# A mixture-of-experts block with two layer norms: the normalising of the second norm is split into a row of subs and a row of muls, with the expert's output matmuls between them

## The chip, the cores and the metric

The kernel runs on the 8 NeuronCores of one Trainium2 chip (trn2). Each core computes 4096 of the 32768 tokens; the cores don't exchange data. The metric is the device time of the slowest core in microseconds (us).

## The reference

Inputs: x of 4 x 8192 x 1024, attention weights of 1024 x 1024, a router of 8 x 1024, w1 (1024 x 8192) and w2 (8192 x 1024) of 8 experts.

```python
xp = x @ Wp.T + bp
q, k, v = (xp @ W.T + b for each, 16 heads of 64; q scaled)
# each token attends to itself and its two neighbours (i-1, i, i+1 modulo s)
x = layernorm(x + (softmax(q . k_neighbours) v_neighbours) @ Wo.T + bo)
# experts: sigmoid router, top 2 of 8, weights normalised to sum 1
h = einsum('td,edw->etw', xf, W1e)
a = square(relu(h))
y = einsum('etw,ewd->etd', a, W2e)
out = einsum('etd,te->td', y, cw)
x = layernorm(x + out)
```

## The kernel before, in words

Everything is feature-major: a tile has 128 partitions of features and 512 columns of tokens, and 8 such chunks (NCH) make up the 1024 features. The kernel has three parts: the weights Wp and Wq, Wk, Wv are multiplied together; eight slabs of 512 tokens go through attention and the first norm, whose result (r1n) is stored to HBM; then come the experts with the second norm, the part that the change touches.

The experts run in NPASS = 4 passes of PW = 1024 tokens, each of NTT = 2 tiles of 512 tokens (`tt` 0 and 1). In a pass the loop goes over 8 experts `e` and the 2 tiles. For each (e, tt) the code writes, in this order:

- on TensorE, the gate matmul (L1038), which spreads this expert's gate over all partitions, and 64 matmuls of h (L1051): 8 chunks, each a sum over 8 matmuls, into two PSUM banks in turn (`ps_hh`);
- on ScalarE, the relu of each chunk (L1058) into one of two buffers of `t1u`; on VectorE the product with the gate (L1063) and with the relu itself (L1067) into `a_sb`;
- then `emit_y` of the *previous* (e, tt): 64 matmuls (L880) with w2, 8 chunks into two PSUM banks in turn (`ps_yy`). For each chunk VectorE copies it to `y_acc` (L889, for e = 0) or adds it (L892), which frees the bank.

The weights of one expert are in `w1e` and `w2e`, 2 MB each in SBUF, one buffer each. `stream_w2(e)` follows the emit_y of the last tile of expert e-1, `stream_w1(e + 1)` follows the h of the last tile of expert e. Both are issued by GpSimd (POOL), which first waits until all earlier loads of its own have landed (`ldb`).

The second norm of a pass is not done at its end. It is cut into pieces that are put in a list, `ln2_pending` (L1103 to L1107), and each (e, tt) of the next pass takes one group off it:

- at (e 0, tt 0), behind emit_y of the last tile of the old pass: `seg_ln2_a` of tile 0 (VectorE adds the residual to y_acc, L912; ScalarE casts it, L918; TensorE sums it with a vector of ones, L923; VectorE squares the cast, L927; TensorE sums the squares, L932; eight times) and `seg_ln2_b_chain` (mean, variance and reciprocal root on one partition: L943 to L949 on VectorE, L954 to L961 on ScalarE);
- at (e 0, tt 1): `seg_ln2_b_bcast` of tile 0 (two matmuls, L968 and L972, spread mean and root over the partitions; ScalarE copies them to `ln2mb`, L978 and L980), `seg_ln2_c` of tile 0 (for each of 8 chunks on VectorE a sub, L995, y_acc less mean into `ln2t`, and a mul, L1000, into `otok`; then SyncE issues the 2 MB store, L1009), `seg_ln2_a` and the chain of tile 1; only then emit_y of (e 0, tt 0);
- at (e 1, tt 0): broadcast and `seg_ln2_c` of tile 1, and then emit_y of (e 0, tt 1).

The norm of the last pass follows behind the last emit_y, with nothing beside it.

Each engine executes its instructions in the order in which the code writes them. emit_y for e = 0 overwrites y_acc of a tile, so it waits until the sub of that tile and chunk has read it (L883 to L886). At the end of expert 1, `load_slice` puts the load of the next pass's r1n (2 MB, L160 on SyncE) behind the stores in SyncE's queue; it waits until they have landed. Pass 3 has no next slice. Before every VectorE instruction that touches a tensor which an earlier one wrote, the helper `_maybe_drain` puts a drain.

I call the three places where a new pass begins turns. At the first one tile 0 is at 1748 us of the trace.

Of the kernel before, what the change touches and what calls it, by code (L numbers as in the profile page):

```python
# [8 lines left out]
BF16 = mybir.dt.bfloat16  # L9
# [5 lines left out]
NCH = 8  # L15
# [3 lines left out]
TT = 512  # L19
# [79 lines left out]
def build_program(T):  # L99
# [3 lines left out]
    PW = T // NPASS  # L103
    NTT = PW // TT
# [40 lines left out]
    p = _Prog(block)  # L145
# [47 lines left out]
    psb = lambda name, shape, dt: ph.enter_context(nc.sbuf_tensor(name, shape, dt)).ap()  # L193
# [16 lines left out]
    for xi, (wxt_h, c_sb, cb_sb, scale) in enumerate(  # L210
# [4 lines left out]
        for dc in range(NCH):  # L215
            for jg in range(2):
# [3 lines left out]
                for kc in range(NCH):  # L220
# [3 lines left out]
                             lambda En, o=role.t, l=lhs, r=rhs, a=(kc == 0), b=(kc == NCH - 1):  # L224
# [5 lines left out]
                          lambda En, o=dst, i_=role.t, sc=scale:  # L230
# [3 lines left out]
        for jc in range(NCH):  # L234
            psfb.wait_writer(p)
            p.wait("tensor", s_ld, base_ld)
            for kc in range(NCH):
                lhs = wxt[:, kc * 1024 + jc * 128: kc * 1024 + jc * 128 + 128]
                v = p.do("tensor",
                         lambda En, o=psfb.t, l=lhs, r=bpb[:, kc:kc + 1],  # L240
                         a=(kc == 0), b=(kc == NCH - 1):
# [5 lines left out]
                      lambda En, o=cb_sb[:, jc:jc + 1], i_=psfb.t, bb=bcol, sc=scale:  # L247
# [469 lines left out]
    ln2scr = psb("ln2scr", [128, 2 * 512], BF16)  # L717
    ln2bc = psb("ln2bc", [128, 2 * 512], BF16)
    ln2mb = psb("ln2mb", [128, 2 * 512], BF16)
    ln2t = psb("ln2t", [128, 2 * 512], BF16)  # L720
    tpk = psb("tpk", [128, 32], F32)
    selp = psb("sel_sb", [E, E * 128], BF16)
    ps_gb = _PsumRole(pst("ps_gb", [128, 512], F32))
# [134 lines left out]
    def stream_w2(e):  # L858
        ldb()
        if w_free[1] is not None:  # L860
            p.wait("gpsimd", *w_free[1])
        dma("gpsimd", w2e.rearrange("p (c n) -> p c n", n=1024),
            w2[e * 1024:(e + 1) * 1024, :].rearrange("(c p) n -> p c n", p=128),
            s_ld, writes=[_h(w2e)])
        return s_ld.n
# [117 lines left out]
        ps_b[2].consumed(s_act, va)  # L983
        ln2st["v_mb"] = va

    def seg_ln2_c(Hh_, tt):
        tok0 = Hh_ * PW + tt * TT
        p.wait("vector", s_act, ln2st["v_mb"])
        if otok_free[0] is not None:
            p.wait("vector", *otok_free[0])  # L990
        for dc in range(NCH):
            ysrc = y_acc[:, dc * PW + tt * TT: dc * PW + tt * TT + TT]
            t_ = ln2t[:, (dc % 2) * 512:(dc % 2) * 512 + 512]
            v_sub = p.do("vector",
                         lambda En, o=t_, a=ysrc: En.tensor_sub(o, a, ln2mb[:, 0:512]),  # L995
                         reads=[_h(y_acc), _h(ln2mb)], writes=[_h(ln2t)], inc=s_dve)
            ln2_freed[(tt, dc)] = (v_sub, ln2st["v_casts"])
            p.do("vector",
                 lambda En, o=otok[:, dc * 512:(dc + 1) * 512], a=t_:
                 En.tensor_mul(o, a, ln2mb[:, 512:1024]),  # L1000
                 reads=[_h(ln2t), _h(ln2mb)], writes=[_h(otok)], inc=s_dve)
        v_otok = s_dve.n
        ln2mb_guard[0] = v_otok
        p.wait("sync", s_dve, v_otok)
        p.do("sync",
             lambda En,
             o=out_h.rearrange("p (c t) -> p c t", t=T)[:, :, tok0: tok0 + TT],
             i_=otok[:, 0:NCH * 512].rearrange("p (c t) -> p c t", t=512):
             En.dma_start(out=o, in_=i_),  # L1009
             inc=s_hw, inc_by=16)  # L1010
        state["n_store"] += 1
        otok_free[0] = (s_hw, s_hw.n)
# [7 lines left out]
    for Hh in range(NPASS):  # L1020
        rp = Hh % 2
        v_w1 = stream_w1(0)
        if Hh == 0:
            v_w2 = stream_w2(0)
            pending = None
        v_h_last = 0
        for e in range(E):
            for tt in range(NTT):
                tok0 = Hh * PW + tt * TT
                apar = (e * NTT + tt) % 2  # L1030
                gbank = ps_gb if apar == 0 else ps_b[0]
                gbank.wait_writer(p)
                if e == 0 and tt == 0:
                    p.wait("tensor", s_dve, gates_ready[Hh])
                v_gb = p.do("tensor",
                            lambda En, o=gbank.t, l=selp[:, e * 128:(e + 1) * 128],
                            r=gates[:, tok0: tok0 + TT]:
                            En.matmul(o[:], l, r, start=True, stop=True), inc=s_pe)  # L1038
                p.wait("tensor", s_ld, v_w1)
                if a_free[apar] is not None:  # L1040
                    p.wait("vector", *a_free[apar])
                for hdc in range(NCH):
                    role = ps_hh[hdc % 2]
                    role.wait_writer(p)
                    for kc in range(NCH):
                        lhs = w1e[:, kc * 1024 + hdc * 128: kc * 1024 + hdc * 128 + 128]
                        rhs = r1n_ps[:, rp * NCH * PW + kc * PW + tt * TT: rp * NCH * PW + kc * PW + (tt + 1) * TT]
                        v = p.do("tensor",
                                 lambda En, o=role.t, l=lhs, r=rhs,
                                 a=(kc == 0), b=(kc == NCH - 1):  # L1050
                                 En.matmul(o[:], l, r, start=a, stop=b),  # L1051
                                 inc=(s_pe if kc == NCH - 1 else None))
                    p.wait("scalar", s_pe, v)
                    t1 = t1u[:, (hdc % 2) * 512:(hdc % 2) * 512 + 512]
                    u = t1u[:, 1024 + (hdc % 2) * 512: 1024 + (hdc % 2) * 512 + 512]
                    if t1_free[hdc % 2] is not None:
                        p.wait("scalar", *t1_free[hdc % 2])
                    va = p.do("scalar", lambda En, o=t1, i_=role.t: En.activation(o, i_[:], AF.Relu),  # L1058
                              reads=[_h(role.t)], writes=[_h(t1u)], inc=s_act)
                    role.consumed(s_act, va)  # L1060
                    p.wait("vector", s_act, va)
                    p.wait("vector", s_pe, v_gb)
                    p.do("vector", lambda En, o=u, a=t1, gb_=gbank.t: En.tensor_mul(o, a, gb_[:]),  # L1063
                         reads=[_h(t1u), _h(gbank.t)], writes=[_h(t1u)], inc=s_dve)
                    vb = p.do("vector",
                              lambda En, o=a_sb[:, apar * NCH * 512 + hdc * 512: apar * NCH * 512 + (hdc + 1) * 512],
                              a=u, b=t1: En.tensor_mul(o, a, b),  # L1067
                              reads=[_h(t1u)], writes=[_h(a_sb)], inc=s_dve)
                    t1_free[hdc % 2] = (s_dve, vb)
                gbank.consumed(s_dve, vb)  # L1070
                if tt == NTT - 1:
                    v_h_last = s_pe.n
                prev = pending
                boundary = (prev is not None and prev[5] == E - 1
                            and prev[3] == NTT - 1)
                if boundary:
                    emit_y(prev)
                    w_free[1] = (s_pe, s_pe.n)
                    v_w2 = stream_w2(0)
                if ln2_pending:  # L1080
                    for f in ln2_pending.pop(0):
                        f()
                if prev is not None and not boundary:
                    emit_y(prev)
                    if prev[5] == e - 1 and prev[3] == NTT - 1 and e > 0:
                        w_free[1] = (s_pe, s_pe.n)
                        v_w2 = stream_w2(e)
                pending = (apar, vb, v_w2, tt, Hh, e)
            if e == 1 and Hh + 1 < NPASS:
                if Hh >= 1:  # L1090
                    slice_guard[(Hh + 1) % 2] = [(s_pe, h_done[Hh - 1]),
                                                 (s_dve, r2_done[Hh - 1])]
                load_slice(Hh + 1)
            if e == 3 and Hh + 1 < NPASS:
                seg_router(Hh + 1)
                gates_ready[Hh + 1] = s_dve.n
            if e + 1 < E:
                w_free[0] = (s_pe, v_h_last)
                v_w1 = stream_w1(e + 1)
        h_done[Hh] = v_h_last  # L1100
        w_free[0] = (s_pe, v_h_last)
        mk = lambda fn, tt: (lambda Hh_=Hh, tt_=tt: fn(Hh_, tt_))
        ln2_pending = [[mk(seg_ln2_a, 0), mk(seg_ln2_b_chain, 0)]]  # L1103
        for t_ in range(1, NTT):
            ln2_pending.append([mk(seg_ln2_b_bcast, t_ - 1), mk(seg_ln2_c, t_ - 1),
                                mk(seg_ln2_a, t_), mk(seg_ln2_b_chain, t_)])
        ln2_pending.append([mk(seg_ln2_b_bcast, NTT - 1), mk(seg_ln2_c, NTT - 1)])  # L1107
    emit_y(pending)
    pending = None
    for grp in ln2_pending:  # L1110
        for f in grp:
            f()

    p.wait("sync", s_hw, s_hw.n)
# [74 lines left out]
```

How the kernel before makes its waits and increments, by code:

```python
    def wait(self, eng, sem, val):  # L39
        if val <= 0:
            return
        self.ops[eng].append(lambda E, s=sem, v=val: E.wait_ge(s.h, v))
# [10 lines left out]
    def do(self, eng, fn, reads=(), writes=(), inc=None, inc_by=1):  # L53
        self._maybe_drain(eng, tuple(reads), tuple(writes))
        if inc is None:
            self.ops[eng].append(lambda E, f=fn: f(E))
        else:
            inc.n += inc_by
            self.ops[eng].append(lambda E, f=fn, s=inc, k=inc_by: f(E).then_inc(s.h, k))
        for h in writes:
            self.dirty[eng].add(id(h))
        for h in reads:
            self.read[eng].add(id(h))
        return inc.n if inc is not None else None
```

## Time and profile before

| | us |
|---|---|
| median of 2 runs | 3494.83 |
| the two runs | 3466.35 and 3523.31 |
| profiled execution | 3476.52 |
| its span, slowest core (4) | 3475.0 |
| spans of the eight cores | 3446.3 to 3475.0 |
| TensorE busy | 2780.9 (80%) |
| VectorE busy | 1506.9 (43%) |
| ScalarE busy | 784.8 (23%) |

The span goes from the first to the last instruction of a core; the time holds 1.5 us more around it. PE is TensorE, DVE is VectorE, ACT is ScalarE, POOL is GpSimd, SP is SyncE. A row of a timeline has the start and the length in us, engine, line, operation, the tensor written and those read, how many were merged, and in brackets how long the engine stood idle before it and what released it.

### The profile page before, as it was taken

What the parts mean: (1) busy time and instruction counts of PE and PEld (TensorE: products, weight loads), DVE (VectorE), ACT (ScalarE), POOL (GpSimd) and SP (SyncE); (2) the same over time, 40 slices, a digit from 0 to 9 for tenths busy, and PEclk for the clock granted to TensorE, in tenths of its full rate; (3) what the DMA queues carried; (4) which work ended last, traced back from release to release, by engine and by line L of the source; (5) the groups of instructions that cost most, each with busy time, mean ns of one, the idle gap of its engine ahead of it and who ended that gap; (6) DMA issues with size and microseconds to landing.
All of it is one profiled execution on the core that took longest, in us unless ns stands there. A gap on an engine that the chain in (4) does not pass through costs nothing.

```text
span 3475.0 us, 43311 instructions; the slowest of 8 cores (3446.3 to 3475.0 us)
## 1 busy us (share of the span) xinstructions
PE 2780.9 (80%) x13408; PEld 1288.5 (37%) x13600; DVE 1506.9 (43%) x2794; ACT 784.8 (23%) x1379; POOL 89.4 (3%) x127
## 2 busy tenths in 40 slices
PE   3577778777876499899868989967989986999992
PEld 1255435443542144344323434423434432444440
DVE  0002443344336344444464444455444446444445
ACT  1134334433442111111221111121111112111111
POOL 1000000000000000000000000000000000000000
PEclk9788888887886699999979999978999997999985
DMA  3410100110000533252425524433325242442511
GB/s 51 73 19 13 25 13 13 25 25 13 13 19 13 109 60 63 49 96 51 73 49 108 86 49 70 77 73 87 59 49 95 51 73 49 93 78 50 86 35 49
DMA packets 98764, 189.71 MB, mean 55 GB/s; under 512 B 3256, under 2 KB 11448, under 8 KB 98544
## 3 DMA queue, kind: packets, MB, share of 16 engines
q0 software_dynamic: 77744, 153.38, 26.4%
q1 hardware_dynamic: 20800, 33.56, 3.0%
q8 instruction: 119, 1.95, 0.2%
q14 instruction: 101, 0.83, 0.1%
HBM read 315.05 MB, written 25.17 MB: 98 GB/s over the span
## 4 chain that ended last, share of the span: by engine, by line
PE 55%; DMA 23%; DVE 8%; issue 5%; ACT 4%; DVEq 2%; ACTq 1%; POOLq 0%; POOL 0%; SPq 0%
PE ps_y L880 19%; PE ps_h L1051 16%; DMA w2e<-w 11%; PE ps_mm L401 10%; DMA w1e<-w 8%; PE ps_mm L551 3%; PE ps_f L225 3%; DVEq L49 2%; DMA xbt<-xs 2%; PE ps_s L445 2%; DVE y_acc L912 1%; DVE otok L1000 1%; ACT wbe L503 1%; DVE ln2t L995 1%; ACT ln2scr L918 1%
## 5 line engine op out<-in xcount | busy, mean ns | idle before, releaser
L880 PE MATMUL ps_y<-a_sb,w2e 128*128 128x512 bf16 x4010 | 916.7, 387 | 98.0 <-DMA w2e<-w 41.8
L1051 PE MATMUL ps_h<-r1n_ps,w1e 128*128 128x512 bf16 x4014 | 915.4, 387 | 34.4 <-DMA w1e<-w 25.4
L1058 ACT ACTIVATE t1u<-ps_h 128x512 bf16<-128x512 f32 x512 | 305.6, 597 | 1544.1 <-PE ps_h L1051 1487.4
L880 PEld LDWEIGHTS ps_y<-a_sb,w2e 128*128 128x128 bf16 x4096 | 405.0, 99 | 604.2 <-issue 166.4
L1051 PEld LDWEIGHTS ps_h<-r1n_ps,w1e 128*128 128x128 bf16 x4096 | 402.0, 99 | 534.3 <-issue 95.5
L892 DVE TENSOR_TENSOR y_acc<-y_acc,ps_y 128x512 f32<-128x512 f32 x448 | 307.6, 687 | 471.4 <-PE ps_y L880 462.8
L1063 DVE TENSOR_TENSOR t1u<-t1u,ps_gb 128x512 bf16<-128x512 bf16 x256 | 176.0, 687 | 238.5 <-ACT t1u L1058 236.9
L1063 DVE TENSOR_TENSOR t1u<-t1u,ps_b 128x512 bf16<-128x512 bf16 x256 | 175.9, 687 | 193.8 <-ACT t1u L1058 193.1
L1067 DVE TENSOR_TENSOR a_sb<-t1u 128x512 bf16<-128x512 bf16 x512 | 217.6, 425 | 47.9 <-issue 0.9
L551 PE MATMUL ps_mm<-k_sb,wot_sb 128*128 128x512 bf16 x496 | 137.8, 442 | 34.1 <-DVE pscr L524 27.2
L225 PE MATMUL ps_f<-wxt_sb,wp_sb 128*128 128x512 bf16 x376 | 89.3, 400 | 85.2 <-DMA wxt_sb<-wqt 48.1
L519 DVE TENSOR_TENSOR pscr<-wbe,v_sb 128x512 bf16<-128x512 bf16 x64 | 26.8, 418 | 262.5 <-ACT wbe L503 262.5
L923 PE MATMUL ps_b<-ln2scr,onesv 128*1 128x512 bf16 x64 | 36.7, 574 | 128.7 <-ACT ln2scr L918 128.7
L401 PE MATMUL ps_mm<-x_fm,ckt 128*128 128x257 bf16 x1024 | 119.0, 275 | 14.5 <-ACT k_sb L407 14.0
L401 PE MATMUL ps_mm<-x_fm,cvt 128*128 128x257 bf16 x1024 | 116.9, 273 | 0.5 <-ACT v_sb L407 0.3
L401 PE MATMUL ps_mm<-x_fm,cqt 128*128 128x257 bf16 x1024 | 116.6, 273 | 0.3 <-ACT q_sb L407 0.3
L401 PEld LDWEIGHTS ps_mm<-x_fm,ckt 128*128 128x128 bf16 x1024 | 92.9, 98 | 41.3 <-issue 19.5
L401 PEld LDWEIGHTS ps_mm<-x_fm,cvt 128*128 128x128 bf16 x1024 | 91.6, 97 | 24.5 <-issue 1.3
L401 PEld LDWEIGHTS ps_mm<-x_fm,cqt 128*128 128x128 bf16 x1024 | 91.5, 97 | 24.1 <-issue 0.5
L551 PEld LDWEIGHTS ps_mm<-k_sb,wot_sb 128*128 128x128 bf16 x512 | 55.8, 109 | 116.1 <-issue 71.6
L434 DVE TENSOR_TENSOR pscr<-q_sb,k_sb 128x512 bf16<-128x512 bf16 x128 | 51.4, 422 | 86.4 <-ACT q_sb L407 55.6
L225 PEld LDWEIGHTS ps_f<-wxt_sb,wp_sb 128*128 128x128 bf16 x384 | 38.9, 102 | 134.3 <-issue 93.9
(153 smaller groups left out, 1665.0 us busy)
## 6 DMA issues: line engine op xcount, KB each, us to landing
w1e<-w POOLq DMA_DIRECT2D x32, 2048.0 KB, 14.7
w2e<-w POOLq DMA_DIRECT2D x32, 2048.0 KB, 15.2
out<-otok SPq DMA_DIRECT2D x8, 2048.0 KB, 7.2
xbt<-xs POOLq DMA_DIRECT2D x32, 256.0 KB, 3.8
r1n_hbm<-r1n_stg SPq DMA_DIRECT2D x8, 1024.0 KB, 5.1
r1n_ps<-r1n_hbm SPq DMA_DIRECT2D x4, 2048.0 KB, 15.8
wp_sb<-wp POOLq DMA_DIRECT2D x1, 2048.0 KB, 16.7
wxt_sb<-wqt POOLq DMA_DIRECT2D x1, 2048.0 KB, 17.4
```

Source lines behind the costliest of these rows:

```text
L49: self.ops[eng].append(lambda E: E.drain())
L225: En.matmul(o[:], l, r, start=a, stop=b),
L401: En.matmul(o[:, 0:w_], l, r, start=a, stop=b),
L434: En.tensor_mul(o_, a, b),
L445: En.matmul(ot[0:NH, :], l, r, start=a, stop=b),
L551: En.matmul(o[:], l, r, start=a, stop=b),
L880: En.matmul(o[:], l, r, start=a, stop=b),
L892: va = p.do("vector", lambda En, o=ydst, i_=role.t: En.tensor_add(o, o, i_[:]), reads=[_h(role.t), _h(y_acc)], writes=[_h(y_acc)], inc=s_dve)
L1051: En.matmul(o[:], l, r, start=a, stop=b),
L1058: va = p.do("scalar", lambda En, o=t1, i_=role.t: En.activation(o, i_[:], AF.Relu), reads=[_h(role.t)], writes=[_h(t1u)], inc=s_act)
L1063: p.do("vector", lambda En, o=u, a=t1, gb_=gbank.t: En.tensor_mul(o, a, gb_[:]), reads=[_h(t1u), _h(gbank.t)], writes=[_h(t1u)], inc=s_dve)
L1067: a=u, b=t1: En.tensor_mul(o, a, b),
```

## The change

`seg_ln2_c` becomes two functions: `seg_ln2_c_subs` writes all 8 subs into `ln2t`, which grows from 2 to 8 chunks for it, and `seg_ln2_c_muls` writes the 8 muls and the store. A group of `ln2_pending` becomes a pair: `pre` is written ahead of emit_y (broadcast and subs), `post` behind it (muls and store; for tile 0 also the statistics and the chain of tile 1). At (e 0, tt 0) the group stays whole and stays behind the emit_y of the old pass. The wait for the store that last used `otok` moves from the subs to the muls.

```diff
-    ln2t = psb("ln2t", [128, 2 * 512], BF16)
+    ln2t = psb("ln2t", [128, 8 * 512], BF16)
...
-    def seg_ln2_c(Hh_, tt):
-        tok0 = Hh_ * PW + tt * TT
+    def seg_ln2_c_subs(Hh_, tt):
         p.wait("vector", s_act, ln2st["v_mb"])
-        if otok_free[0] is not None:
-            p.wait("vector", *otok_free[0])
         for dc in range(NCH):
...
-            t_ = ln2t[:, (dc % 2) * 512:(dc % 2) * 512 + 512]
+            t_ = ln2t[:, dc * 512:(dc + 1) * 512]
...
+    def seg_ln2_c_muls(Hh_, tt):
+        tok0 = Hh_ * PW + tt * TT
+        if otok_free[0] is not None:
+            p.wait("vector", *otok_free[0])
+        for dc in range(NCH):
             p.do("vector",
...
-                if ln2_pending:
-                    for f in ln2_pending.pop(0):
-                        f()
+                for f in pre:
+                    f()
                 if prev is not None and not boundary:
                     emit_y(prev)
...
+                for f in post:
+                    f()
...
+        ln2_pending = [([mk(seg_ln2_a, 0), mk(seg_ln2_b_chain, 0)], [])]
         for t_ in range(1, NTT):
+            ln2_pending.append(([mk(seg_ln2_b_bcast, t_ - 1), mk(seg_ln2_c_subs, t_ - 1)],
+                                [mk(seg_ln2_c_muls, t_ - 1),
+                                 mk(seg_ln2_a, t_), mk(seg_ln2_b_chain, t_)]))
+        ln2_pending.append(([mk(seg_ln2_b_bcast, NTT - 1), mk(seg_ln2_c_subs, NTT - 1)],
+                            [mk(seg_ln2_c_muls, NTT - 1)]))
```

TensorE in the kernel before, at a turn, from the broadcast of tile 0 (L968) on; the pair L923, L932 stands there eight times, and L880 is emit_y of (e 0, tt 0):

```order
L968 MATMUL ps_b<-stb,onescol 128x512
L972 MATMUL ps_b<-stb,onescol 128x512
L923 MATMUL ps_b<-ln2scr,onesv 1x512
L932 MATMUL ps_b<-ln2bc,onesv 1x512
...
L880 MATMUL ps_y<-a_sb,w2e 128x512 x64
L1038 MATMUL ps_gb<-gates,sel_sb 128x512
L1051 MATMUL ps_h<-r1n_ps,w1e 128x512 x64
```

The same place after the change (L1042 and L1055 are the old L1038 and L1051):

```order
L968 MATMUL ps_b<-stb,onescol 128x512
L972 MATMUL ps_b<-stb,onescol 128x512
L880 MATMUL ps_y<-a_sb,w2e 128x512 x64
L923 MATMUL ps_b<-ln2scr,onesv 1x512
L932 MATMUL ps_b<-ln2bc,onesv 1x512
...
L1042 MATMUL ps_gb<-gates,sel_sb 128x512
L1055 MATMUL ps_h<-r1n_ps,w1e 128x512 x64
```

emit_y has moved ahead of the statistics matmuls of tile 1, which now stand directly before the h of expert 1. On TensorE nothing else has moved.

VectorE before, at tile 0 of a turn; L995 and L1000 are sub and mul, eight times in turn, L912 and L927 the statistics of tile 1:

```order
L1067 TENSOR_TENSOR a_sb<-t1u 128x512
L995 TENSOR_TENSOR ln2t<-y_acc,ln2mb 128x512
L1000 TENSOR_TENSOR otok<-ln2t,ln2mb 128x512
...
L912 TENSOR_TENSOR y_acc<-y_acc,r1n_ps 128x512
L927 TENSOR_TENSOR ln2bc<-ln2scr 128x512
```

VectorE there after the change (L1071 is the old L1067, L992 the sub, L1004 the mul):

```order
L1071 TENSOR_TENSOR a_sb<-t1u 128x512
L992 TENSOR_TENSOR ln2t<-y_acc,ln2mb 128x512 x8
L889 COPY y_acc<-ps_y 128x512 x8
L1004 TENSOR_TENSOR otok<-ln2t,ln2mb 128x512 x8
L912 TENSOR_TENSOR y_acc<-y_acc,r1n_ps 128x512
L927 TENSOR_TENSOR ln2bc<-ln2scr 128x512
```

The eight copies of emit_y, which stood behind the statistics and the chain of tile 1, are now between subs and muls. At tile 1 it is likewise subs, copies, muls, and then the products of the next h (L1067); before it was subs and muls in turn, copies, products. The orders of ScalarE, GpSimd and SyncE are the same before and after.

## Rows read from the trace of the kernel before

**Rows 1.** The chain that ended last, by engine.

```profile
PE 55%; DMA 23%; DVE 8%; issue 5%; ACT 4%; DVEq 2%; ACTq 1%; POOLq 0%; POOL 0%; SPq 0%
```

**Rows 2.** Timeline of TensorE, first turn, tile 0.

```profile
1748.08 0.39 PE L968 MATMUL ps_b<-stb,onescol 1*128 1x512 bf16 x1
...
1764.22 0.58 PE L923 MATMUL ps_b<-ln2scr,onesv 128*1 128x512 bf16 x1 [15.54 <-ACT ln2scr L918]
...
1780.70 15.82 PE L880 MATMUL ps_y<-a_sb,w2e 128*128 128x512 bf16 x62 [0.33 <-issue]
...
1810.69 0.39 PE L968 MATMUL ps_b<-stb,onescol 1*128 1x512 bf16 x1
```

**Rows 3.** Timeline of VectorE, first turn, tile 0: first sub, first statistics add.

```profile
1750.28 0.68 DVE L995 TENSOR_TENSOR ln2t<-y_acc,ln2mb 128x512 bf16<-128x512 f32 x1
...
1762.63 0.68 DVE L912 TENSOR_TENSOR y_acc<-y_acc,r1n_ps 128x512 f32<-128x512 f32 x1
```

**Rows 4.** Timeline of TensorE, first turn, tile 1 and what follows.

```profile
1811.23 3.63 PE L880 MATMUL ps_y<-a_sb,w2e 128*128 128x512 bf16 x16
1826.07 1.44 PE L880 MATMUL ps_y<-a_sb,w2e 128*128 128x512 bf16 x3 [11.22 <-DVE y_acc L889]
...
1838.07 0.38 PE L1038 MATMUL ps_b<-gates,sel_sb 8*128 8x512 bf16 x1
1838.39 13.99 PE L1051 MATMUL ps_h<-r1n_ps,w1e 128*128 128x512 bf16 x62
1859.36 15.94 PE L880 MATMUL ps_y<-a_sb,w2e 128*128 128x512 bf16 x63 [6.99 <-DMA w2e<-w]
...
1875.55 13.99 PE L1051 MATMUL ps_h<-r1n_ps,w1e 128*128 128x512 bf16 x63
```

**Rows 5.** Timeline of VectorE, first turn, tile 1.

```profile
1812.89 0.68 DVE L995 TENSOR_TENSOR ln2t<-y_acc,ln2mb 128x512 bf16<-128x512 f32 x1
...
1825.24 1.47 DVE L889 COPY y_acc<-ps_y 128x512 f32<-128x512 f32 x2
...
1838.42 0.69 DVE L889 COPY y_acc<-ps_y 128x512 f32<-128x512 f32 x1 [1.04 <-PE ps_y L880]
```

**Rows 6.** Stretches: PE, PEld, DVE, ACT, POOL busy, granted clock, DMA share, GB/s.

```profile
1815.00:1819.00 4.00, 0.00 (x0) 0.00 (x0) 3.54 (x6) 0.00 (x0) 0.00 (x0) 1.00 0.00 0
1819.00:1829.00 10.00, 2.71 (x6) 1.05 (x8) 6.88 (x11) 0.00 (x0) 0.00 (x0) 0.50 0.24 88
```

**Rows 7.** Timeline of TensorE, first turn, behind the statistics of tile 0.

```profile
1731.01 0.60 PE L1038 MATMUL ps_b<-gates,sel_sb 8*128 8x512 bf16 x1
...
1737.63 10.52 PE L1051 MATMUL ps_h<-r1n_ps,w1e 128*128 128x512 bf16 x47 [1.43 <-ACT t1u L1058]
```

**Rows 8.** SyncE's issues and all DMA issues of 1820:1900 with us to landing.

```profile
1825.41 0.58 SPq L1009 DMA_DIRECT2D out<-otok  x1
1833.64 0.57 SPq L160 DMA_DIRECT2D r1n_ps<-r1n_hbm  x1
...
out<-otok SPq DMA_DIRECT2D x1, 2048.0 KB, 8.1
r1n_ps<-r1n_hbm SPq DMA_DIRECT2D x1, 2048.0 KB, 14.3
w2e<-w POOLq DMA_DIRECT2D x1, 2048.0 KB, 20.4
w1e<-w POOLq DMA_DIRECT2D x1, 2048.0 KB, 13.0
```

**Rows 9.** DMA issues of 2968:2990, third turn, with us to landing.

```profile
w2e<-w POOLq DMA_DIRECT2D x1, 2048.0 KB, 15.5
w1e<-w POOLq DMA_DIRECT2D x1, 2048.0 KB, 15.2
```

**Rows 10.** GpSimd's issue of w1e in the first turn, with us to landing.

```profile
1748.93 0.87 POOL L160 DMA_DIRECT2D w1e<-w  x1 [34.77 <-PE ps_b L972]
...
w1e<-w POOLq DMA_DIRECT2D x1, 2048.0 KB, 14.9
```

More of the change, by code:

```diff
@@ L997, in seg_ln2_c @@
             ln2_freed[(tt, dc)] = (v_sub, ln2st["v_casts"])
+    def seg_ln2_c_muls(Hh_, tt):
[3 more added lines that the diff above has]
+        for dc in range(NCH):
             p.do("vector",
-                 lambda En, o=otok[:, dc * 512:(dc + 1) * 512], a=t_:
+                 lambda En, o=otok[:, dc * 512:(dc + 1) * 512],
+                 a=ln2t[:, dc * 512:(dc + 1) * 512]:
                  En.tensor_mul(o, a, ln2mb[:, 512:1024]),
@@ L1075, in build_program @@
                             and prev[3] == NTT - 1)
+                pre, post = ln2_pending.pop(0) if ln2_pending else ((), ())
                 if boundary:
@@ L1102, in build_program @@
         mk = lambda fn, tt: (lambda Hh_=Hh, tt_=tt: fn(Hh_, tt_))
-        ln2_pending = [[mk(seg_ln2_a, 0), mk(seg_ln2_b_chain, 0)]]
+        ln2_pending = [([mk(seg_ln2_a, 0), mk(seg_ln2_b_chain, 0)], [])]
         for t_ in range(1, NTT):
-            ln2_pending.append([mk(seg_ln2_b_bcast, t_ - 1), mk(seg_ln2_c, t_ - 1),
-                                mk(seg_ln2_a, t_), mk(seg_ln2_b_chain, t_)])
-        ln2_pending.append([mk(seg_ln2_b_bcast, NTT - 1), mk(seg_ln2_c, NTT - 1)])
+            ln2_pending.append(([mk(seg_ln2_b_bcast, t_ - 1), mk(seg_ln2_c_subs, t_ - 1)],
[3 more added lines that the diff above has]
+                            [mk(seg_ln2_c_muls, NTT - 1)]))
     emit_y(pending)
     pending = None
-    for grp in ln2_pending:
-        for f in grp:
+    for pre, post in ln2_pending:
+        for f in pre:
+            f()
+        for f in post:
             f()
```

## Prediction

> **What bounds the kernel now.** I read the page's chain of waits first, then the timelines of TensorE, VectorE and SyncE around one turn from a pass of experts to the next, then the DMA issues there. In the chain [rows 1] the reader is to see that TensorE's own work is 55% and DMA 23%: the kernel is an alternation of matmuls and weight loads, and VectorE is on the chain with only 8%. That 8% is the second layer norm. There are four passes. The norm of each of the first three is worked off at the start of the next pass, that of the last at the end. The edit changes the order of instructions only in the three turns. In the last norm it only sorts the same 16 VectorE instructions of a tile otherwise, with nothing beside them.
>
> I call a broadcast (L968) the start of a tile's normalising. For tile 0 [rows 2] TensorE issues it at 1748.08, then stands almost still: 15.54 us before the first statistics matmul of tile 1, and only at 1780.70 does it start emit_y of expert 0. The next broadcast, of tile 1, is at 1810.69, so this stretch takes 62.6 us. VectorE [rows 3] works through 16 subs and muls from 1750.28 to 1762.63: 12.35 us, 0.77 us each. For tile 1 [rows 4] TensorE does two chunks of emit_y (3.63 us), finds both PSUM banks full, and waits 11.22 us for VectorE's y_acc copy, which stands behind another 16 subs and muls [rows 5].
>
> **Tile 0, part by part.** The same 16 instructions exist after the change, each writing a tensor used by the one before it, so I keep 0.77 us for each; splitting them into 8 subs and 8 muls is 6.2 us and 6.2 us. Counted from the broadcast:
> TensorE starts emit_y at 0.6 and fills two banks by 4.2. The subs begin at 2.2 and end at 8.4. The first copy then frees a bank 0.8 us later (1825.24 to 1826.07, rows 4 and 5), so TensorE goes on at 9.2. The other six chunks took 12.0 us after such a wait (1826.07 to 1838.07) [rows 4]; at full speed they are six eighths of 13.99 us, 10.5. I take 12.0, since the wait of 5 us left over is near the point at which the clock falls: in tile 1 the granted clock was 1.00 up to 1819, 4 us into a wait, and then 0.50 (1.2 GHz) for 10 us [rows 6]. TensorE is through at 21.2, the last copy at 22.3 (it starts 0.35 after the matmul, rows 5, and takes a slot of 0.77). The muls end at 28.5.
> Then comes what now follows the muls, the statistics of tile 1: 1762.63 to 1780.70, 18.1 us, to 46.6. Behind it the h matmuls run cold and their relu stands behind ScalarE's four small operations of chain. The trace has exactly that sequence after tile 0's statistics: from the gate matmul at 1731.01, with a wait of 1.43, to the broadcast at 1748.08, 17.1 us [rows 7]. Sum 63.7, against 62.6 before: **1.0 us lost**, in each of three turns 3.0. The 8 subs hidden under emit_y are paid back because emit_y no longer covers chain and the cold clock. If the clock stays up in emit_y, 0.5 is gained instead.
>
> **Tile 1.** The same steps bring TensorE through emit_y at 21.2 after the broadcast, where it was at 27.4 (1838.07 less 1810.69): 6.2 us earlier. The muls are now ahead of the next h phase on VectorE, for 6.2 us. There the relu may run two chunks ahead, so TensorE loses some 1.7 us (two chunks of 1.75 and two of relu against 6.2 and the backlog). That is hidden: the h phase is followed by a wait for w2e anyway, 6.99 us here [rows 4], which h at 14.0 + 1.7 doesn't fill.
>
> So what counts is the chain of transfers: emit_y frees w2e, POOL loads it (and issues the next w1e only when it has landed), and the next h waits for w1e. Here lies the cost that isn't in the code. Before, the store of the outputs was issued at 1825.41, landed after 8.1 us, and the load of the next slice followed at 1833.64, still ahead of w2e at 1838.7 [rows 8]. w2e then took 20.4 us against 15.5 us in the third turn, where no slice is loaded [rows 9]: a transfer beside it cost 4.9. After the change w2e is issued 21.8 us after the broadcast and the store at 28.5, when the muls end: the whole 2 MB store now falls inside w2e's load, and the slice load, which stands behind the store in SyncE's queue, falls on the w1e load.
> - Store beside w2e: between 0 (the store waits) and 8.1 us (w2e waits for all of it); I take 4.5, near the 4.9 of the slice. w2e lands 20.0 after its issue.
> - Slice beside w1e: w1e alone takes 15.2 [rows 9]. The slice began 5 us ahead of w2e and cost it 4.9; begun together the two share for longer. Bounds 0 and 14.3 (the slice's own time, rows 8); I take 7.
> First and second turn, from the end of emit_y to the h matmuls of expert 2: before 1838.07 to 1875.55, 37.5 us. After: 0.6 + 20.0 + 1.0 (issue) + 15.2 + 7 = 43.8, 6.3 more. Less the 6.2 gained, 0.1 lost; and that h runs cold after a wait of some 8 us (12.0 less 10.5 above), 1.5 more: **1.6 lost**, twice 3.2. Third turn: 6.2 less 4.5 for the store: **1.7 gained** (w1e's load is as before).
> Sum: 3.0 + 3.2 - 1.7 = 4.5 us slower, on 3476.5 us of the profiled execution (span 3475.0): **3481 us**. That lies inside the two runs shown (3466 and 3523, median 3494.8), and 0.13% is far below the 2% that a measurement of this kernel can tell from no change.
>
> **The page's rules against this.** The slice row shows that two transfers of different queues share: both moved, both were late. The Trainium skill (DMA: Bandwidth & Descriptors, Queues, rings and completion order) says that each DMA engine takes turns between queue rows, packet by packet. By it the store would cost w2e no more than the store's own share, which is between my bounds; the trace agrees with the 4.9 us.
> A second result: w2e is now issued just ahead of the 8 muls, and POOL writes its descriptors while VectorE reads two SBUF operands. If that held the load up for as long as the muls last, each turn would lose 6.2 us more, 18.6 in all. The only row on it is w1e's load at 1748.9, issued 1.4 us ahead of the same subs and muls: it landed after 14.9 us [rows 10], no later than w1e's 15.2 without them. So I give it little. The Trainium skill (SBUF — State Buffer, Who interferes with whom) states that a VectorE instruction with two SBUF inputs contends with a GpSimd instruction that reads SBUF, though not with one that only writes; the row speaks against a cost here.
>
> **The rivals.**
> 1. Nothing collides, faster. Store and slice find room, the clock stays up: tile 0 gains 3 x 0.5, tile 1 3 x 6.2, together 20.1, so 3456 us; with the 4.9 of w2e's old delay recovered twice (and 37.5 before against 0.6 + 15.5 + 1.0 + 15.2 = 32.3), up to 10 more, 3446. For it: DMA is idle for long stretches, and 11.22 us of wait are plainly visible. Against: the store's issue time follows from the order, 6.7 us into a load of 15.5.
> 2. The pile-up decides, slower. SyncE issues the slice at about the moment POOL issues w1e, after the store and w2e landed together. If w1e gets nothing until the slice is through, it takes 14.3 + 13.0 = 27.3 (rows 8), 5.1 more than I took, twice; with the store at 5.5 instead of 4.5, three more: 4.5 + 10.2 + 3 = 17.7, 3494 us. It decides from the point at which the store lands before w2e does. Against: in rows 8 two loads finished 11 us apart, so both made way.
> 3. Descriptors held up by the muls: 4.5 + 18.6 = 23.1, 3500 us. Against: rows 10.
> 4. The edit does nothing, because VectorE in its order is the only bound: 3476.5. It is within 5 us of my forecast and can't be told from it by time, only by the waits.
>
> **How the numbers follow.** Forecast 0.55 (with rival 4 in it), rival 1 0.2, rival 2 0.2, rival 3 0.05. The cases lie between 3446 and 3500; each carries the scatter of the executions, of which two and the profiled one span 3466 to 3523. Range 3450 to 3512: it holds all the cases but the end of rival 1, and leaves out the top of the scatter. 2% would be 70 us, which no case reaches: within 2% 0.94; slower 0.04, for scatter on rivals 2 and 3; faster 0.02.
>
> **What would show it.** Right: in each turn the wait for y_acc L889 about 5 us instead of 11, and now also in tile 0 (six such waits, three before); 24 to 26 us of TensorE at rest or in statistics after emit_y of tile 0; broadcast to broadcast 62 to 64 us; w2e(1) landing after about 20 us in all three turns; w1e(2) after 20 us or more in the first two, with TensorE waiting 6 to 9 us for it. Wrong: if w2e(1) lands after 15.5 us beside the store, or w1e(2) after 13 to 15 beside the slice (rival 1 then); if w1e(2) takes 27 (rival 2); if w2e(1) starts moving only when the muls have ended (rival 3); if subs in a row take less than 0.77 us each.

## The result and the profile after

The changed kernel takes 3476.5 us (median of 15 runs), the kernel before 3467.0 us (median of 14 runs, the two shown above among them). The ratio is 1.0028, 95% interval 1.0019 to 1.0037: 9.7 us slower, 6.6 to 12.8. That is clear of noise and far below 2%. In some executions of either kernel one die shows a lower granted clock and takes longer; the ratio leaves these out, 3523.3 was one, and the profiled execution before leans that way (cores 4 to 7: clock 0.879, 3464 to 3475 us; cores 0 to 3: 0.884, 3446 to 3457 us). So 3467, close to the lower of the two runs shown above, is the time to start from, and not 3494.8 or 3476.5.

The profiled execution after has a span of 3471.5 us on core 2. Its waits of TensorE, in us in total, times, longest:

```profile
PE ps_b L923 <- ACT ln2scr L918: 108.2, 64, 15.5
...
PE ps_y L880 <- DMA w2e<-w: 40.5, 19, 5.3
PE ps_h L1055 <- DMA w1e<-w: 35.2, 21, 5.9
PE ps_y L880 <- DVE y_acc L889: 31.2, 6, 5.6
```

The wait for the copy is there six times, each of 5 us, instead of three times 11.22 [rows 4]: as forecast, in sum almost the same. TensorE now also waits for w1e, up to 5.9 us on this core and up to 13.1 us on core 7.

Timeline of TensorE on core 2 in the first turn after, from the broadcast of tile 0 on (statistics matmuls left out):

```profile
1751.39 0.39 PE L968 MATMUL ps_b<-stb,onescol 1*128 1x512 bf16 x1
...
1751.93 3.63 PE L880 MATMUL ps_y<-a_sb,w2e 128*128 128x512 bf16 x15
1760.69 12.67 PE L880 MATMUL ps_y<-a_sb,w2e 128*128 128x512 bf16 x47 [5.14 <-DVE y_acc L889]
...
1798.39 0.60 PE L1042 MATMUL ps_gb<-gates,sel_sb 8*128 8x512 bf16 x1
1798.92 5.44 PE L1055 MATMUL ps_h<-r1n_ps,w1e 128*128 128x512 bf16 x16
1805.09 10.52 PE L1055 MATMUL ps_h<-r1n_ps,w1e 128*128 128x512 bf16 x47 [0.72 <-ACT t1u L1062]
1815.54 0.38 PE L968 MATMUL ps_b<-stb,onescol 1*128 1x512 bf16 x1
...
1824.84 13.02 PE L880 MATMUL ps_y<-a_sb,w2e 128*128 128x512 bf16 x47 [5.14 <-DVE y_acc L889]
1837.79 0.38 PE L1042 MATMUL ps_b<-gates,sel_sb 8*128 8x512 bf16 x1
1838.11 7.08 PE L1055 MATMUL ps_h<-r1n_ps,w1e 128*128 128x512 bf16 x32
1846.91 7.07 PE L1055 MATMUL ps_h<-r1n_ps,w1e 128*128 128x512 bf16 x31 [1.72 <-ACT t1u L1062]
1859.30 16.31 PE L880 MATMUL ps_y<-a_sb,w2e 128*128 128x512 bf16 x63 [5.32 <-DMA w2e<-w]
1875.54 0.39 PE L1042 MATMUL ps_gb<-gates,sel_sb 8*128 8x512 bf16 x1
1881.83 15.30 PE L1055 MATMUL ps_h<-r1n_ps,w1e 128*128 128x512 bf16 x63 [5.90 <-DMA w1e<-w]
```

There are three things to see. emit_y of tile 0 stands ahead of the statistics, with its wait of 5.14. The h that follows the statistics (1798.39 to 1815.54, 17.2 us) is the slow one, as in [rows 7]; the granted clock is 0.68 from 1798.4 to 1805 and 1.00 after it. And the two waits for transfers stand behind tile 1.

The DMA issues of that turn after on core 2, with us to landing, which answer to [rows 8]:

```profile
w2e<-w POOLq DMA_DIRECT2D x1, 2048.0 KB, 20.6
out<-otok SPq DMA_DIRECT2D x1, 2048.0 KB, 16.7
w1e<-w POOLq DMA_DIRECT2D x1, 2048.0 KB, 21.7
r1n_ps<-r1n_hbm SPq DMA_DIRECT2D x1, 2048.0 KB, 21.2
```

Both collisions of the forecast are here: the store needs 16.7 us instead of 8.1 and w2e 20.6, the slice 21.2 instead of 14.3 and w1e 21.7 instead of 13.0. But w2e took 20.4 before as well, beside the slice: in this turn the store has only taken the slice's place, and what is new is the delay of w1e. And the cores differ. Core 0, the same turn after:

```profile
w2e<-w POOLq DMA_DIRECT2D x1, 2048.0 KB, 15.6
out<-otok SPq DMA_DIRECT2D x1, 2048.0 KB, 13.8
w1e<-w POOLq DMA_DIRECT2D x1, 2048.0 KB, 25.7
```

On cores 0, 3, 5 and 7 w2e lands after 15.4 to 15.9 us although the store is beside it, in all three turns; there w1e pays, with 24.4 to 26.6 us in the first two turns and 18.1 to 18.6 in the third, where the end of the store falls into its load. On cores 1, 2, 4 and 6 w2e takes 18.4 to 21.3 and w1e 21.7 to 23.9 (15.3 to 16.9 in the third). Why the cores fall into two groups stays open. Means of the eight cores:

| us to landing | before | after |
|---|---|---|
| w2e, turns 1 and 2 | 18.0 | 17.6 |
| w1e, turns 1 and 2 | 14.3 | 24.0 |
| w2e, turn 3 | 14.4 | 17.5 |
| w1e, turn 3 | 15.4 | 17.1 |

To add up, I measured these distances in the timelines of all eight cores and took their means:

| us, mean of 8 cores | before | after | difference | forecast |
|---|---|---|---|---|
| broadcast tile 0 to broadcast tile 1, per turn | 61.7 | 63.7 | +2.0 | +1.0 |
| broadcast tile 1 to end of emit_y, per turn | 28.3 | 22.4 | -5.9 | -6.2 |
| from there to expert 2's second tile, turns 1 and 2 | 63.6 | 73.0 | +9.4 | +7.8 |
| the same, turn 3 | 59.9 | 65.3 | +5.4 | +4.5 |

Three times 2.0 less three times 5.9, and 2 x 9.4 and 5.4: 12.3 us before rounding on these two executions. On cores 0 to 3 alone the distances add up to 13.0 us, and the mean span of these four cores grew by 12.8 us. By the runs it is 9.7 (6.6 to 12.8); why the slowest core of a run loses some 3 us less stays open.

### The profile page after: what moved, and what is told of

Same layout as the page of the kernel before. It is cut to its first block, busy times and chain, and to the rows that moved or that the text cites. A ratio compares the mean times of both kernels' runs of the same rounds, so it can differ in the third digit from the quotient of the medians.

```text
span 3471.5 us, 43311 instructions; the slowest of 8 cores (3458.1 to 3471.5 us)
## 1 busy us (share of the span) xinstructions
PE 2782.5 (80%) x13408; PEld 1288.0 (37%) x13600; DVE 1507.2 (43%) x2794; ACT 785.2 (23%) x1379; POOL 89.4 (3%) x127
## 4 chain that ended last, share of the span: by engine, by line
PE 54%; DMA 25%; DVE 8%; issue 5%; ACT 4%; DVEq 2%; ACTq 1%; POOLq 0%; POOL 0%; another core or an unknown queue 0%; SPq 0%
PE ps_y L880 17%; PE ps_h L1055 16%; DMA w2e<-w 11%; PE ps_mm L401 10%; DMA w1e<-w 9%; PE ps_mm L551 3%; PE ps_f L225 3%; DVEq L49 2%; DMA xbt<-xs 2%; PE ps_s L445 2%; DVE y_acc L912 1%; ACT wbe L503 1%; ACT ln2scr L918 1%; ACTq L49 1%; DVE ln2t L992 1%
## 5 line engine op out<-in xcount | busy, mean ns | idle before, releaser
L880 PE MATMUL ps_y<-a_sb,w2e 128*128 128x512 bf16 x4010 | 917.0, 387 | 95.0 <-DMA w2e<-w 40.5
L1055 PE MATMUL ps_h<-r1n_ps,w1e 128*128 128x512 bf16 x4014 | 911.7, 385 | 50.2 <-DMA w1e<-w 35.2
L880 PEld LDWEIGHTS ps_y<-a_sb,w2e 128*128 128x128 bf16 x4096 | 404.2, 99 | 602.0 <-issue 144.0
L1055 PEld LDWEIGHTS ps_h<-r1n_ps,w1e 128*128 128x128 bf16 x4096 | 400.4, 99 | 549.3 <-issue 96.0
L1067 DVE TENSOR_TENSOR t1u<-t1u,ps_gb 128x512 bf16<-128x512 bf16 x256 | 176.1, 688 | 242.6 <-ACT t1u L1062 237.1
L1067 DVE TENSOR_TENSOR t1u<-t1u,ps_b 128x512 bf16<-128x512 bf16 x256 | 176.1, 688 | 178.5 <-ACT t1u L1062 176.7
L1071 DVE TENSOR_TENSOR a_sb<-t1u 128x512 bf16<-128x512 bf16 x512 | 217.7, 425 | 47.8 <-issue 0.9
L401 PE MATMUL ps_mm<-x_fm,ckt 128*128 128x257 bf16 x1024 | 120.2, 277 | 14.6 <-ACT k_sb L407 14.1
L923 PE MATMUL ps_b<-ln2scr,onesv 128*1 128x512 bf16 x64 | 36.6, 573 | 108.2 <-ACT ln2scr L918 108.2
L918 ACT CAST ln2scr<-y_acc 128x512 bf16<-128x512 f32 x64 | 39.5, 617 | 255.2 <-DVE y_acc L912 255.2
## 6 DMA issues: line engine op xcount, KB each, us to landing
w1e<-w POOLq DMA_DIRECT2D x32, 2048.0 KB, 14.8
w2e<-w POOLq DMA_DIRECT2D x32, 2048.0 KB, 15.3
wxt_sb<-wqt POOLq DMA_DIRECT2D x1, 2048.0 KB, 17.7
```

Of the source, the lines that this page charges most:

```text
L401: En.matmul(o[:, 0:w_], l, r, start=a, stop=b),
L918: vc = p.do("scalar", lambda En, o=rb, i_=ydst: En.copy(o, i_), reads=[_h(y_acc)], writes=[_h(ln2scr)], inc=s_act)
```

## The experiments

All ratios are to the kernel before, run beside it on the same chip; e1 to e4, e5 to e8, and e9 with e10 are on three different chips, so a difference between two of these groups is one between two ratios. The theory is that the loss comes from two transfers that the late muls have moved; the rivals are tile 0 (cold clock, lost cover) and VectorE's muls themselves.

**e1: only tile 0 is split.**

```diff
-        ln2_pending.append(([mk(seg_ln2_b_bcast, NTT - 1), mk(seg_ln2_c_subs, NTT - 1)],
-                            [mk(seg_ln2_c_muls, NTT - 1)]))
+        ln2_pending.append(([mk(seg_ln2_b_bcast, NTT - 1), mk(seg_ln2_c_subs, NTT - 1),
+                             mk(seg_ln2_c_muls, NTT - 1)], []))
```

> Only tile 0 of a turn is split; at tile 1 subs, muls, copies follow as subs and muls did before. The theory of the transfers (the loss is the store beside the load of w2e and the slice beside the load of w1e, both set off by tile 1's late muls) expects the small loss of tile 0 alone: 1.4 us from broadcast to broadcast per turn, 4 us in all slower than the kernel before, w2e(1) and w1e(2) in 20.5 and 13 us as before. The rival (the loss is emit_y's cold clock and a norm that no longer hides behind emit_y, so it sits in tile 0) expects nearly all of the loss, 8 to 10 us.

Measured: ratio 1.0020 (1.0010 to 1.0030), 6.9 us slower (3.5 to 10.4). That is between the two expectations, and by the time alone either could stand. The trace decides: the stretch from broadcast to broadcast is 63.7 us (mean of 8 cores), 2.0 longer than before and not 1.4, and behind tile 1 nothing changed (62.9 and 63.4 us in the first two turns, 58.9 in the third). Tile 0 is a loss, three times 2.0, but not all of it.

**e2: only tile 1 is split.**

```diff
-            ln2_pending.append(([mk(seg_ln2_b_bcast, t_ - 1), mk(seg_ln2_c_subs, t_ - 1)],
-                                [mk(seg_ln2_c_muls, t_ - 1),
-                                 mk(seg_ln2_a, t_), mk(seg_ln2_b_chain, t_)]))
+            ln2_pending.append(([mk(seg_ln2_b_bcast, t_ - 1), mk(seg_ln2_c_subs, t_ - 1),
+                                 mk(seg_ln2_c_muls, t_ - 1),
+                                 mk(seg_ln2_a, t_), mk(seg_ln2_b_chain, t_)], []))
```

> Only tile 1 of a turn is split. The theory of the transfers expects emit_y to end 5.6 us earlier in each of three turns (16.8), against 2 x 8.6 us from expert 1's end to expert 2 in the first two turns and 4.7 in the third: 5 us slower than the kernel before. The rival (tile 0 carries the loss) expects tile 1 to be pure gain, 10 to 17 us faster than before.

Measured: 1.0007 (0.9997 to 1.0018), 2.4 us slower (-1.0 to 6.2). The rival, which had tile 1 as a gain of 10 to 17 us, falls. emit_y ends 22.2 us after the broadcast as in the changed kernel, and the way behind it is 72.5, 72.3 and 65.0 us in the three turns: what tile 1 wins, the transfers take. The two halves add up: 6.9 + 2.4 = 9.3 against 9.7, each with several us of uncertainty.

**e3: the changed kernel with the slice load one expert earlier**, and so ahead of tile 1's store in SyncE's queue.

```diff
-            if e == 1 and Hh + 1 < NPASS:
+            if e == 0 and Hh + 1 < NPASS:
                 if Hh >= 1:
...
                 load_slice(Hh + 1)
```

> The changed kernel, but the load of the next slice is issued after expert 0 instead of after expert 1, so SyncE has it ahead of tile 1's store and it moves while the DMA queues are idle. The theory of the transfers expects w1e(2) to land in 15 us instead of 21.7, the first two turns to become like the third (0.5 us from the kernel before's, less the 5 us that the slice cost w2e there): 8 to 9 us faster than the kernel before. The rival theories (VectorE's muls or the clock) expect no change against the changed kernel: 9 to 10 us slower than before.

Measured: 0.9994 (0.9983 to 1.0005), 2.1 us faster than the kernel before and 11.8 faster than the changed one. Core 2, first turn, the DMA issues from tile 1 on:

```profile
w2e<-w POOLq DMA_DIRECT2D x1, 2048.0 KB, 19.6
out<-otok SPq DMA_DIRECT2D x1, 2048.0 KB, 16.1
w1e<-w POOLq DMA_DIRECT2D x1, 2048.0 KB, 14.5
```

w1e lands after 14.5 instead of 21.7, and h of expert 2 begins without a wait. On cores 0, 3 and 6, where w2e is done after 15 to 16 us, w1e still takes 18 to 19 beside the end of the store and TensorE waits 5 to 6 us for it; the mean of the eight cores is 16.7 instead of 24.0. The way behind tile 1 is 63.8 us in the first two turns instead of 73.0, like the third (64.0); without cores 4 and 5, which are quick in this execution (the last section is on such pairs), it is 64.9 and 65.0. So the slice beside w1e is shown as the cause of 8 to 9 us in each of the first two turns by the traces; by the runs the two turns together are 11.8.

Expected were 8 to 9 us against the kernel before, and 2.1 were measured (from 5.9 faster to 1.7 slower). Tile 0 at 2.0 instead of 1.4 explains 1.8 us of that. Another 2.6 are the slice's old cost: I had counted 5 us per turn as won back, but before the change the first two turns are only 3.7 us longer than the third behind tile 1 (63.6 and 59.9). The rest is within the interval.

**e4: the kernel before with the same move.**

> The kernel before with the same move of the slice load. The theory of the transfers expects w2e(1) in 15.5 us instead of 20.4 in two turns: 10 us faster than the kernel before, and so the change itself, with this and e3 compared, to cost about 1 to 2 us. The rival (the slice is hidden in the kernel before, TensorE is the bound there) expects no change.

Measured: 0.9984 (0.9955 to 1.0012): the time alone decides nothing. The trace does. Core 2, first turn:

```profile
w2e<-w POOLq DMA_DIRECT2D x1, 2048.0 KB, 13.4
w1e<-w POOLq DMA_DIRECT2D x1, 2048.0 KB, 15.5
```

w2e lands after 13.4 us, where this core took 19.9 in the kernel before. [Rows 8], with 20.4, are core 4's and lie high: the mean of the eight cores in the first two turns was 18.0 and is now 14.3. The way to expert 2's second tile is 3.5 us shorter (59.5 and 60.6 instead of 63.6), not 5. So the slice cost the kernel before 3.5 to 3.7 us in each of two turns.

**e5: the changed kernel without tile 1's store in the third turn** (outputs of 512 tokens per core are left out). There is no slice load in this turn.

```diff
+        if Hh_ == 2 and tt == 1:
+            return
         p.wait("sync", s_dve, v_otok)
```

> The changed kernel without the store of tile 1 in the third turn (the outputs of 512 tokens per core are left out); the muls stay, and no slice is loaded in this turn. If the store beside it is what slows w2e(1) there, w2e(1) lands after 15.3 us again instead of 18.3 (mean of 8 cores to the next issue) and the way from expert 1 to expert 2 is 60 us instead of 65.3. If VectorE's muls hold up the descriptors, or the transfer suffers from their SBUF traffic, w2e(1) still needs 18 us or more.

One run. Third turn on core 2, the changed kernel first (with the store), then e5:

```profile
w2e<-w POOLq DMA_DIRECT2D x1, 2048.0 KB, 18.5
out<-otok SPq DMA_DIRECT2D x1, 2048.0 KB, 15.1
```

```profile
w2e<-w POOLq DMA_DIRECT2D x1, 2048.0 KB, 15.2
```

The muls stood where they stood, and w2e landed after 15.2 us, like that of [rows 9] of before; the means of the eight cores are 17.5 in the changed kernel, 14.1 in e5 and 14.4 before. So the store is the cause, and neither the descriptors of the load nor the muls' SBUF traffic. The way to expert 2's second tile fell from 65.3 to 61.0 us, while the first two turns, unchanged, stayed at 72 to 73. It did not fall to 60 because one cover is gone. TensorE in e5, third turn:

```profile
2977.30 7.08 PE L1057 MATMUL ps_h<-r1n_ps,w1e 128*128 128x512 bf16 x32
2986.10 7.07 PE L1057 MATMUL ps_h<-r1n_ps,w1e 128*128 128x512 bf16 x32 [1.71 <-ACT t1u L1064]
2993.01 13.97 PE L880 MATMUL ps_y<-a_sb,w2e 128*128 128x512 bf16 x64
```

h with its wait of 1.71 behind the muls now ends after w2e has landed, so emit_y starts with no wait for w2e, and the next w1e, whose buffer h must have left, is issued 17.0 us after the end of emit_y. In the kernel before it was issued after 15.1 to 16.9 us there.

**e6: both transfers out of the way.** e3, and tile 1's store of a turn is issued when w1e(2) has landed.

```diff
+        if Hh_ + 1 < NPASS and tt == NTT - 1:
+            late_store.append(store)
+        else:
+            store()
...
                 v_w1 = stream_w1(e + 1)
+                if e == 1 and late_store:
+                    p.wait("sync", s_ld, v_w1)
+                    late_store.pop(0)()
```

> The changed kernel with both transfers out of the way: the slice load after expert 0, as in e3, and tile 1's store of a turn issued only when w1e(2) has landed. The theory of the transfers expects w2e(1) in 15.3 us in all turns and 5 us less per turn than e3: 14 to 17 us faster than e3, some 17 us faster than the kernel before (0.5%). The rival (the store's transfer is hidden, muls on VectorE delay) expects the time of e3.

Measured: 0.9946 (0.9932 to 0.9960), 18.7 us faster than the kernel before. 17 were expected. So with the transfers out of the weight loads' way the same order wins, where with them it lost. Not all of the half per cent is the order's: the early slice alone gave the kernel before a ratio of 0.9984 (e4, 0.9955 to 1.0012). Against e4 the order is worth 13 us by the runs, 10 us by the distances of the two traces (8 without the two quick cores of e6).

**e7 and e9: e6 with each mul directly behind the copy of the same chunk.**

```diff
             role.consumed(s_dve, va)
+            if fill is not None:
+                fill(ydc)
...
-                    emit_y(prev)
+                    emit_y(prev, seg_mul if has_c else None)
```

> e6 with each mul written directly behind the copy of the same chunk of emit_y, where VectorE waits 1.03 us per chunk. If VectorE's order is what is exposed at tile 0, the 6.2 us of muls vanish from each broadcast-to-broadcast stretch (63.7 to 57.5 us, mean of 8 cores) and the h phase at tile 1 no longer waits 1.7 us: 18 us faster than e6, 1.0% faster than before. If emit_y's own matmuls or the cold clock set the pace there, less than half of that.

These runs gave no ratio; in the trace the stretch from broadcast to broadcast is 58.4 us (mean of cores 0 to 3) instead of 63.7. The same kernel again:

> The kernel of e7 once more, since few of its runs there could be used. By its trace a turn is 13 us shorter than in the kernel before (206.3 against 218.4 us on the way from the turn's first gate matmul to expert 2's second tile, mean of cores): the theory of VectorE's order expects 36 to 40 us faster than before, a ratio of 0.989. The rival (the rest of the gain is given back elsewhere) expects the ratio of e6, 0.9946.

Measured: 0.9906 (0.9873 to 0.9939), 32.5 us faster than before. The 0.989 expected lies inside the interval and e6's 0.9946 outside it, if only just. (The expectation's 206.3 against 218.4 us is 12 us per turn and not 13.) VectorE there, core 0:

```profile
1761.35 0.69 DVE L889 COPY y_acc<-ps_y 128x512 f32<-128x512 f32 x1 [0.44 <-PE ps_y L880]
1761.95 0.68 DVE L1006 TENSOR_TENSOR otok<-ln2t,ln2mb 128x512 f32<-128x512 bf16 x1
1763.07 0.69 DVE L889 COPY y_acc<-ps_y 128x512 f32<-128x512 f32 x1 [0.44 <-PE ps_y L880]
```

The mul lies in the pause that VectorE has between two chunks: 0.44 us of idle time are left of 1.03 [rows 5 show 1.04], and the copies still come every 1.72 us.

**e8: the statistics woven in too.** For each chunk of emit_y VectorE does copy, add, mul and square; TensorE's two sums follow one chunk later. It applies at both places where statistics stood alone, and where the last pass ends.

```diff
+        def fill(dc):
+            add_cast(dc)
+            if dc >= 1:
+                sums(dc - 1)
+            if muls:
+                seg_mul(dc)
+            square(dc)
+        emit_y(st_, fill)
+        sums(NCH - 1)
```

> e7 with the statistics of a tile also between the chunks of emit_y (VectorE: copy, add, mul, square per chunk, 2.8 us; TensorE's two sums one chunk later), at both places where they stood alone, and so in the last norm. The theory that TensorE only waits for VectorE in a turn expects tile 0's stretch to fall to about 42 us from 57, the statistics of tile 0 to cost 5 us instead of 18: 25 us per turn and 13 at the end less, 80 to 90 us faster than e7. If PSUM banks and the order of sums and chunks stall emit_y, only half of it.

Measured: 0.9731 (0.9716 to 0.9747), 93 us faster than the kernel before and 61 faster than e9. It beats both kernels. The expectation was 80 to 90 over the kernel of e7 and e9. Broadcast to broadcast is 50.8 us, not 42: I had left the broadcast and the eight subs (8.4 us) out of that number. VectorE, core 0, tile 0:

```profile
1761.22 0.69 DVE L889 COPY y_acc<-ps_y 128x512 f32<-128x512 f32 x1
1762.00 0.69 DVE L912 TENSOR_TENSOR y_acc<-y_acc,r1n_ps 128x512 f32<-128x512 f32 x1
1762.61 0.69 DVE L1035 TENSOR_TENSOR otok<-ln2t,ln2mb 128x512 f32<-128x512 bf16 x1
1763.60 0.42 DVE L925 TENSOR_TENSOR ln2bc<-ln2scr 128x512 bf16<-128x512 bf16 x1 [0.30 <-ACT ln2scr L918]
1764.11 0.69 DVE L889 COPY y_acc<-ps_y 128x512 f32<-128x512 f32 x1
```

One chunk takes 2.89 us (1761.22 to 1764.11), the four operations and 0.30 of waiting for ScalarE's cast: here VectorE is the bound, and TensorE's 1.90 us of emit_y per chunk lie beside it.

**e10: e8 with the two transfers where the change has them.**

> The kernel of e8 with both transfers where the change has them: the slice load behind expert 1, the store of tile 1 at once. The theory of the transfers expects it to lose again what e6 won over the changed kernel, 9 us in each of the first two turns and 4 to 5 in the third: 20 to 28 us slower than e8, a ratio of 0.979 to 0.981 to the kernel before. The rival (with other work so much shorter, the transfers find their own room) expects the ratio of e8, 0.973.

Measured: 0.9836 (0.9821 to 0.9851), so the two transfers cost 1.05% or 36 us here, more than the 20 to 28 expected (e8 and e10 are on two chips; the distances of the two traces give 34 to 36). Core 2, first turn, from 1811 us:

```profile
w2e<-w POOLq DMA_DIRECT2D x1, 2048.0 KB, 20.2
out<-otok SPq DMA_DIRECT2D x1, 2048.0 KB, 20.3
w1e<-w POOLq DMA_DIRECT2D x1, 2048.0 KB, 22.7
r1n_ps<-r1n_hbm SPq DMA_DIRECT2D x1, 2048.0 KB, 23.0
```

The muls now end with emit_y, so store and w2e start together and end together, on every core (w2e 18.5 to 21.0 us, store 18.8 to 21.2). From the end of emit_y to expert 2's first gate it is 37.0 us (mean of eight cores) against 29.0 in e8, in all three turns; the changed kernel, whose store started 7 us into the load, has 33.5. To expert 2's second tile it is 73.0 in the first two turns and 65.3 in the third, the same as in the changed kernel, where e8 has 58.5 and 58.0. So the same two transfers cost more here (36 us) than between the changed kernel and e6 (28 us).

## Why the prediction came out as it did

The direction and the mechanism were right, and the size was not: 4.5 us were forecast, 9.7 (6.6 to 12.8) measured. Both waits of 5 us, the 17.1 us of h behind the statistics (17.2) and the 1.7 us of h behind the muls (1.72) are in the trace, and on core 2 also w2e in 20.0 (20.6) and w1e in 22.2 (21.7).

**The step that failed** is the size of two terms, "1.0 us lost" for tile 0 and "6.3 more" for the way behind tile 1, and in both it is the side of the kernel before. In both, the length before was read from the first turn of core 4, and that turn is longer than most. The length after was right, or nearly:

| us | before, core 4, first turn | before, mean of 8 cores | after, forecast | after, measured |
|---|---|---|---|---|
| broadcast to broadcast | 62.6 | 61.7 | 63.7 | 63.7 |
| end of emit_y to the h of expert 2, turns 1 and 2 | 37.5 | 35.3 | 43.8 | 43.3 |

So "1.0 us lost" measures 2.0 and "6.3 more" measures 8.0; with the 1.4 that this h then runs longer (1.5 forecast) the second gives the 9.4 of the table above. The distances add up to 12.3 us against the 4.5 of the forecast. Of the 7.8 between them tile 0 is 3.0 (three times 1.0) and the way behind tile 1 in turns 1 and 2 is 3.2; the rest is 0.8 for emit_y of tile 1 and 0.9 for turn 3. The same turn on core 2 before, to be read beside [rows 2]:

```profile
1745.03 0.39 PE L968 MATMUL ps_b<-stb,onescol 1*128 1x512 bf16 x1
1777.68 14.77 PE L880 MATMUL ps_y<-a_sb,w2e 128*128 128x512 bf16 x62 [0.33 <-issue]
1806.61 0.39 PE L968 MATMUL ps_b<-stb,onescol 1*128 1x512 bf16 x1
```

It takes 61.6 us. Up to the start of emit_y it is the same 32.6; emit_y takes 14.77 instead of 15.82. In its first 4 us the granted clock was 0.75 here and 0.50 on core 4.

That 3476.5 lies so near the forecast of 3481 is luck: the base was 9.5 us too high (3476.5 instead of 3467.0), and the difference 5.2 us too small.

The terms, and the rivals:

- **Tile 0, "1.0 us lost".** Measured 2.0, in the changed kernel and in e1, where tile 0 alone is split (63.7 there too).
- **Tile 1, 6.2 us earlier.** Measured 5.9. The six chunks behind the wait took 12.67 and 13.02 us on core 2, not 12.0.
- **"A transfer beside it cost 4.9".** That was core 4 again: over the eight cores w2e before took 18.0 in turns 1 and 2 and 14.4 in turn 3, a difference of 3.6.
- **Turns 1 and 2, "6.3 more" and 1.5 of cold clock.** Measured 8.0 and 1.4. How the loads share the delay was right on four cores only: the means of the eight are 17.6 for w2e (20.0 forecast) and 24.0 for w1e (22.2). On the other four the sign named for "wrong", w2e landing after 15.5 beside the store, is there, and yet rival 1 doesn't hold, because w1e is the later for it.
- **Turn 3, 4.5 for the store.** Measured 5.4: w2e 3.1 later and w1e 1.7.
- **"That is hidden", the 1.7 us of h behind the muls.** True on core 2 and the three like it, where w2e is slow. On the four cores with a quick w2e, w2e lands at about the time h ends, and in e5 before it, so there those 1.7 us are not hidden.
- **Rival 1 (nothing collides)** was wrong for the changed kernel, and its size too: e6 makes it true by hand, with the slice moved as well, and gives 18.7 us, where 20 to 30 stood.
- **Rival 2 (the pile-up decides)** gave 17.7 us and w1e in 27.3. w1e came to 26.6 at the most, on one core, and the time to 12.8 at the most: it is out as a whole, though four cores come near it with 24.4 to 26.6.
- **Rival 3 (descriptors held up)** fell with e5, as [rows 10] had suggested. The Trainium skill (SBUF — State Buffer, Who interferes with whom) names GpSimd instructions that read SBUF as what a VectorE instruction with two SBUF inputs contends with; by the 15.2 us with the muls beside it, the making of this load's descriptors is none.
- **Taking turns.** In e10 two transfers of 2 MB that start together land after 20.2 and 20.3 us, where they need 15.2 and 8.1 alone. The Trainium skill (DMA: Bandwidth & Descriptors, Queues, rings and completion order) has each engine alternate between queue rows by packets; this pair agrees. The one that matters loses 5 us to the one that doesn't. For a store that starts 7 us into the load the runs give no such simple share: four cores show w2e delayed by 3 to 6 us, four show it hardly delayed at all.
- **Rival 4 (no effect)** is out by the interval, whose lower end is 6.6 us.

## What to carry to other kernels

When an edit moves the end of a chain that triggers a transfer, write down where each transfer behind it will fall and what it will meet; here the same reordering was worth +0.28% with its store and the next slice landing on the weight loads, and -0.54% with them moved (some 0.2% of which the moved slice may give by itself). Removing a wait of TensorE's pays little when the work waited for is only done later in the same chain: splitting alone gave little, and putting each mul and each statistics step into the pause between two chunks, with the transfers moved, gave 2.7% (1.6% without moving them). And take the length of a stretch from all turns and cores before subtracting two of them.

## What the runs showed of the hardware that was not expected

In some executions two neighbouring cores are far quicker than the rest, by 50 to 90 us. In e6 the spans of the first die are:

```profile
core 0: 3350.7 us, clock 0.891
core 1: 3374.6 us, clock 0.888
core 2: 3430.1 us, clock 0.885
core 3: 3437.5 us, clock 0.888
```

The DMA issues of core 0 and then of core 2, medians of 32 loads:

```profile
w1e<-w POOLq DMA_DIRECT2D x32, 2048.0 KB, 12.9
w2e<-w POOLq DMA_DIRECT2D x32, 2048.0 KB, 13.6
```

```profile
w1e<-w POOLq DMA_DIRECT2D x32, 2048.0 KB, 15.3
w2e<-w POOLq DMA_DIRECT2D x32, 2048.0 KB, 13.7
```

Core 0 waits 7.1 us in all for weights (4.9 for w2e and 2.2 for w1e), core 2 57.3 (5.9 and 51.4): it waits for w1e 25 times. On the other three pairs one core has w1e in 15.3 to 15.6 and w2e in 13.5 to 13.7, the other 14.7 to 14.8 and 14.8 to 15.1; on cores 0 and 1 both have 12.9 and 13.6. So the difference of 2.4 us in w1e goes with the difference in span. That would fit loads of two neighbouring cores disturbing each other when they fall together, and cores 0 and 1, whose spans differ by 24 us where those of the other pairs differ by 7 to 10, no longer doing so. It was only seen, not tested. The metric, the slowest core, doesn't profit.
